# One run of score chunks a turn over six PSUM banks, with the other banks and the projection pieces dealt anew

## What is computed

```python
q = (x @ Wq).reshape(B, T, H, D)
k = (x @ Wk).reshape(B, T, H, D)
v = (x @ Wv).reshape(B, T, H, D)
q = _rmsnorm(q, q_rms_w)
k = _rmsnorm(k, k_rms_w)
...
gate = jax.nn.softplus(gate_logits)
bias = -dist[None, None] * omega_eff[None, :, None, None] * gate[:, :, None, :]
bias = jnp.where(causal[None, None], bias, -jnp.inf)
scores = jnp.einsum('bihd,bjhd->bhij', q, k) * scale + bias
attn = jax.nn.softmax(scores, axis=-1)
y = jnp.einsum('bhij,bjhd->bihd', attn, v).reshape(B, T, H * D)
return y @ Wproj
...
h = jnp.einsum('bei,eih->beh', jnp.concatenate([merged, ones], -1), w1)
h = jax.nn.gelu(h, approximate=False)
o = jnp.einsum('bej,ejo->beo', jnp.concatenate([h, ones], -1), w2)
```

## Time and profile before

| | us |
|---|---|
| median of 3 runs | 1491.17 |
| lowest and highest of them | 1486.17, 1493.72 |
| the profiled execution | 1487.67 |
| its span in the profile | 1485.9 |
| mean granted TensorE clock over the span | 0.973 of full |

### The profile page before, as it was taken

The page is one execution under the profiler, slowest core; times in us unless marked ns, Lnnn a source line. Parts: engine busy times, 40 slices in busy tenths (PEclk is TensorE's granted clock), DMA queues, the critical chain, the costliest instruction groups (busy, mean ns, idle before and its releaser), DMA issues.

```text
span 1485.9 us, 28161 instructions
## 1 busy us (share of the span) xinstructions
PE 1414.3 (95%) x9680; PEld 1089.7 (73%) x9680; DVE 990.7 (67%) x3164; ACT 914.2 (62%) x2292; POOL 165.5 (11%) x559
## 2 busy tenths in 40 slices
PE   3779999999999999999999999999998899999998
PEld 2566778777877877777777778777775778878787
DVE  5837885888587678757876885878587544444442
ACT  4637785878588577848866784877577433333332
POOL 4501110111011101101110110111011000000000
PEclk9779999999999999999999999999999999999999
DMA  5542322232223222323231322222230311111100
GB/s 202 193 161 79 99 94 80 80 121 71 93 67 108 83 85 76 114 67 102 96 98 61 99 94 80 80 97 84 75 94 6 87 39 40 40 39 40 39 15 29
DMA packets 88303, 122.90 MB, mean 83 GB/s; under 512 B 8561, under 2 KB 74466, under 8 KB 88162
## 3 DMA queue, kind: packets, MB, share of 16 engines
q1 hardware_dynamic: 85554, 116.35, 24.4%
q10 hardware_dynamic: 2608, 4.76, 0.9%
HBM read 101.69 MB, written 19.40 MB: 81 GB/s over the span
## 4 chain that ended last, share of the span: by engine, by line
PE 88%; ACT 4%; DVE 1%; issue 1%; DMA 0%; SPq 0%; ACTq 0%; DVEq 0%
PE at L797 18%; PE at L806 11%; PE at L882 10%; PE at L1467 8%; PE at L857 8%; PE at L923 7%; PE at L1503 6%; PE at L811 3%; PE at L892 2%; PE at L909 2%; PE at L849 2%; PE at L837 2%; PE at L1486 2%; PE at L842 2%; ACT L1063 1%; ACT probT L1054 1%
## 5 line engine op out<-in xcount | busy, mean ns | idle before, releaser
L1045 ACT ACTIVATE prob<-prob,low 128x512 f32<-128x512 f32 (+3 forms) x512 | 280.6, 550 | 70.5 <-DVE low L1178 70.5
L1178 DVE CUSTOM_DVE_ANT_0 prob<-at,mask 128x512 f32<-128x512 f32 (+3 forms) x512 | 220.4, 486 | 78.7 <-PE at L811 78.7
L1054 ACT ACTIVATE probT<-at 128x512 f32<-128x512 f32 (+1 forms) x256 | 131.5, 540 | 123.1 <-PE at L857 123.0
L806 PE MATMUL at<-kT,qT 64*128 64x512 f32 (+3 forms) x1024 | 194.0, 460 | 8.8 <-DVE up_lo L1231 5.0
L797 PE MATMUL at<-w_hi,cT_lo 128*128 128x386 f32 x512 | 197.3, 385 | 5.1 <-DVE area_raw L1127 4.3
L797 PE MATMUL at<-w_hi,cT_hi 128*128 128x386 f32 x512 | 174.8, 342 | 0.0
L797 PE MATMUL at<-w_lo,cT_hi 128*128 128x386 f32 x512 | 174.7, 341 | 0.0
L857 PEld LDWEIGHTS at<-ident,prob 128*128 128x128 f32 x1280 | 142.4, 141 | 40.0 <-issue 36.8
L857 PE MATMUL at<-ident,prob 128*128 128x128 f32 x1280 | 164.4, 275 | 2.1 <-DVE prob L1191 1.9
L1191 DVE TENSOR_SCALAR prob<-prob,rec 128x512 f32<-128x512 f32 (+3 forms) x512 | 163.3, 383 | 4.5
L882 PE MATMUL at<-probT,v 128*64 128x512 f32 (+3 forms) x1024 | 152.8, 440 | 0.1
(11 more groups left out here) (216 smaller groups left out, 2563.4 us busy)
## 6 DMA issues: line engine op xcount, KB each, us to landing
area_w<-in_L_ffn_w SPq DMA_DIRECT2D x64, 1024.0 KB, 5.6
bias<-in_L_ffn_w SPq DMA_DIRECT2D x160, 32.0 KB, 3.7
x_in<-in_L_attn_x SPq DMA_DIRECT2D x8, 512.0 KB, 5.8
xr<-in_L_attn_x SPq DMA_DIRECT2D x8, 512.0 KB, 4.0
eo_d<-eo SPq DMA_DIRECT2D x32, 128.0 KB, 1.8
x_d<-xr SPq DMA_DIRECT2D x8, 512.0 KB, 2.9
area_raw<-x_d SPq DMA_DIRECT2D x8, 512.0 KB, 4.0
out<-area_raw SPq DMA_DIRECT2D x8, 512.0 KB, 2.9
```

What stands on the lines that cost most here:

```text
L806: eng.matmul(bS[i][:, at:at + (c + 1) * P], qT[rows, c * P:(c + 1) * P], kT[rows, 0:(c + 1) * P], start=True, stop=False)
L1045: eng.activation(sl, sl, ACT.Exp, scale=-1.0, bias=low[:, i:i + 1], accum_out=den[:, i:i + 1]).then_inc(exp_done.sem, 1)
L1054: eng.activation(probT[h][:, x:y], bR[i][:, 0:y - x], ACT.Copy).then_inc(done.sem, 1)
L1178: eng.tensor_tensor_reduce(out=prob[s % 2][h][:, off[c]:off[c + 1]], in0=bS[i][:, at:at + (c + 1) * P], in1=mask[:, (NT - 1 - c) * P:T], s ...
```

## The change

All four score chunks of a turn stand in one run on TensorE (`all_scores`), over six banks: the three `bS` and the three `bR` (`bC`). The projection no longer shares a bank with them. The transposed probabilities of head 0 go to `bS`, those of head 1 to `bR`, and each waits until `lows` has emptied its bank of this turn's scores, not until the other head's copies are done. The values' result, the experts' products and the hidden rows take one `bS` bank each (`bY`, `bX`, `bH`). Projection piece 1 moves ahead of `turn_p1`, piece 2 ahead of `values`. VectorE and ScalarE are reordered to match. The run of scores now starts with the waits that `scores_210` had: for `add_bias`, `copy_expert_output` and `copy_hidden` of the turn before.

```diff
-        bY = bR[2]
-        bX = bS[2]
-        bS = bS + [bQ[0]]
+        bY, bX, bH = bS
+        bP = (bS, [bR[2], bR[0], bR[1]])
+        bC = bS + [bR[2], bR[0], bR[1]]
...
         place = {(3, 0): (0, 0), (3, 1): (1, 0), (1, 0): (2, 0), (1, 1): (3, 0),
-                 (2, 0): (1, 0), (2, 1): (0, 0), (0, 0): (1, 3 * P), (0, 1): (0, 3 * P)}
+                 (2, 0): (4, 0), (2, 1): (5, 0), (0, 0): (4, 3 * P), (0, 1): (5, 3 * P)}
...
-                def scores_3(s):
+                def all_scores(s):
                     eng.wait_ge(maxed.sem, maxed.at(s - 1))
-                    scores(3)
-
-                def scores_210(s):
+                    eng.wait_ge(y_done.sem, y_done.at(s - 2))
                     if begins_in(s - 1) is not None:
                         eng.wait_ge(biased.sem, biased.at(begins_in(s - 1)))
                     if s > 1 and ends_in(s - 1) is not None:
                         eng.wait_ge(eo_done.sem, eo_done.at(ends_in(s - 1)))
-                    eng.wait_ge(raw_D.sem, raw_D.at(s + 2 if s + 2 < NTURN else NTURN - 1))
-                    for n in jobs_at.get((s, 1), ()):
-                        eng.wait_ge(prep_done.sem, prep_done.at(n))
-                    scores(1)
-                    eng.wait_ge(maxed.sem, maxed.at(s, 2))
-                    if ends_in(s) is not None:
-                        eng.wait_ge(hidT_done.sem, hidT_done.at(ends_in(s)))
-                    scores(2)
-                    scores(0)
+                        eng.wait_ge(hidT_done.sem, hidT_done.at(ends_in(s - 1)))
+                    for c in (3, 1, 2, 0):
+                        scores(c)
...
                 def turn_p0(s):
                     eng.wait_ge(p_done.sem, p_done.at(s, 1))
                     for i in range(3):
+                        if s + 1 < NTURN:
+                            eng.wait_ge(maxed.sem, maxed.at(s + 1, i + 1))
                         turn_p(s, 0, i)
 
                 def turn_p1(s):
                     eng.wait_ge(p_done.sem, p_done.at(s, 2))
-                    eng.wait_ge(pt0_A.sem, pt0_A.at(s, 1))
-                    turn_p(s, 1, 0)
-                    eng.wait_ge(pt0_D.sem, pt0_D.at(s))
-                    turn_p(s, 1, 1)
-                    eng.wait_ge(pt0_A.sem, pt0_A.at(s, 2))
-                    turn_p(s, 1, 2)
+                    for i in range(3):
+                        if s + 1 < NTURN:
+                            eng.wait_ge(maxed.sem, maxed.at(s + 1, (4, 7, 8)[i]))
+                        turn_p(s, 1, i)
...
                 def hidden(m, s):
-                    eng.wait_ge(maxed.sem, maxed.at(s, 4))
+                    eng.wait_ge(maxed.sem, maxed.at(s, 2))
+                    eng.wait_ge(pt0_D.sem, pt0_D.at(s - 1))
...
                     if s > 0:
                         turn_p0(s - 1)
                     if s + 2 < NTURN:
                         eng.wait_ge(o_done.sem, o_done.at((s - 1) // HP - 1))
                         project(s + 2, 0)
                     prepare(s, 0)
+                    if s + 2 < NTURN:
+                        project(s + 2, 1)
+                    prepare(s, 1)
                     if s > 0:
                         turn_p1(s - 1)
                     if ends_in(s) is not None:
                         turn_hidden(ends_in(s), s)
                     if s + 2 < NTURN:
-                        project(s + 2, 1)
-                    prepare(s, 1)
-                    if s < NTURN:
-                        scores_210(s)
+                        project(s + 2, 2)
+                    prepare(s, 2)
                     if s > 0:
                         values(s - 1)
...
-                    if s < NTURN:
-                        eng.wait_ge(maxed.sem, maxed.at(s, 4))
-                    if s + 2 < NTURN:
-                        project(s + 2, 2)
-                    prepare(s, 2)
                     if s + 1 < NTURN:
+                        if s == 0:
+                            eng.wait_ge(maxed.sem, maxed.at(0, 8))
                         turn_q(s + 1)
```

More of the change, by code:

```diff
@@ L805, in scores @@
                         rows = slice(h * D, (h + 1) * D)
-                        eng.matmul(bS[i][:, at:at + (c + 1) * P], qT[rows, c * P:(c + 1) * P], kT[rows, 0:(c + 1) * P],
+                        eng.matmul(bC[i][:, at:at + (c + 1) * P], qT[rows, c * P:(c + 1) * P], kT[rows, 0:(c + 1) * P],
                                    start=True, stop=False)
@@ L810, in scores @@
                         rows = slice(h * D, (h + 1) * D)
-                        m = eng.matmul(bS[i][:, at:at + (c + 1) * P], qaug[rows, c * P:(c + 1) * P],
+                        m = eng.matmul(bC[i][:, at:at + (c + 1) * P], qaug[rows, c * P:(c + 1) * P],
                                        kaug[rows, 0:(c + 1) * P], start=False, stop=True)
                         m.then_inc(pe_s.sem, 1)
-                def scores_3(s):
+                def all_scores(s):
                     eng.wait_ge(maxed.sem, maxed.at(s - 1))
-                    scores(3)
-                def scores_210(s):
+                    eng.wait_ge(y_done.sem, y_done.at(s - 2))
                     if begins_in(s - 1) is not None:
@@ L955, in _ @@
                         eng.wait_ge(kaug_done.sem, kaug_done.at(s))
-                        scores_3(s)
+                        all_scores(s)
                     else:
                         eng.wait_ge(y_done.sem, y_done.at(s - 2))
+                        eng.wait_ge(eo_done.sem, eo_done.at(E - 1))
                     if s > 0:
@@ L1053, in copy_p @@
                     x, y = segT[i]
-                    eng.activation(probT[h][:, x:y], bR[i][:, 0:y - x], ACT.Copy).then_inc(done.sem, 1)
+                    eng.activation(probT[h][:, x:y], bP[h][i][:, 0:y - x], ACT.Copy).then_inc(done.sem, 1)
                 def copy_y(s):
@@ L1090, in _ @@
                         exps(s, 3)
+                        exps(s, 1)
+                    if s > 0:
+                        copy_p(s - 1, 0, 0)
+                        copy_p(s - 1, 0, 2)
                     prepare(s, 0)
+                    if s + 1 < NTURN:
+                        rsqrt(s + 1)
+                    if s + 2 < NTURN:
+                        take_raw(s + 2, 1)
+                    prepare(s, 1)
                     if s > 0:
@@ L1094, in _ @@
                         copy_p(s - 1, 1, 2)
-                    if s + 1 < NTURN:
-                        rsqrt(s + 1)
                     if s % 4 == 2:
                         exps(s, 3)
-                    prepare(s, 1)
-                    if s + 2 < NTURN:
-                        take_raw(s + 2, 1)
+                        exps(s, 1)
+                    if s < NTURN:
+                        exps(s, 2)
                     if s + 1 < NTURN:
                         gate(s + 1)
+                    if s + 2 < NTURN:
+                        take_raw(s + 2, 2)
+                    prepare(s, 2)
                     if s < NTURN:
-                        exps(s, 1)
-                        exps(s, 2)
                         exps(s, 0)
@@ L1178, in lows @@
                         eng.tensor_tensor_reduce(
-                            out=prob[s % 2][h][:, off[c]:off[c + 1]], in0=bS[i][:, at:at + (c + 1) * P],
+                            out=prob[s % 2][h][:, off[c]:off[c + 1]], in0=bC[i][:, at:at + (c + 1) * P],
                             in1=mask[:, (NT - 1 - c) * P:T], scale=-1.0, scalar=-LOWEST, op0=ALU.add, op1=ALU.min,
@@ L1200, in copy_p @@
                     x, y = segT[1]
-                    eng.tensor_copy(probT[h][:, x:y], bR[1][:, 0:y - x]).then_inc(done.sem, 1)
+                    eng.tensor_copy(probT[h][:, x:y], bP[h][1][:, 0:y - x]).then_inc(done.sem, 1)
                 def add_bias(m):
@@ L1251, in _ @@
                         lows(s, 3)
+                        lows(s, 1)
+                    if s + 1 < NTURN:
+                        mean_square(s + 1)
+                    if s < NTURN:
+                        lows(s, 2)
+                        lows(s, 0)
+                    if s + 2 < NTURN:
+                        take_raw(s + 2)
+                    prepare(s, 0)
                     if s > 0:
                         copy_p(s - 1, 0)
-                    if s + 2 < NTURN:
-                        take_raw(s + 2)
+                    prepare(s, 1)
                     if s + 1 < NTURN:
-                        mean_square(s + 1)
-                    prepare(s, 0)
+                        newton_step(s + 1)
                     if s > 0:
                         copy_p(s - 1, 1)
-                    if ends_in(s) is not None:
-                        copy_hidden(ends_in(s))
                     if s + 1 < NTURN:
-                        newton_step(s + 1)
                         gate_input(s + 1)
@@ L1267, in _ @@
                         gate(s + 1)
-                    prepare(s, 1)
-                    if s < NTURN:
-                        lows(s, 1)
```

(4 more changed lines are left out.)

21 lines of the change are left out of this document (8 added, 13 removed).

## The result

The changed kernel takes 1505.11 us (median of 4 runs, 1501.82 to 1507.73), the kernel before, beside it, 1488.99 (4 runs). The ratio is 1.0104, with a 95% interval of 1.0068 to 1.014: slower by 1.0%, 16.1 us. The forecast was 1502 and slower.

What follows compares the result with a forecast made beforehand. TensorE's own work bounds each turn; other engines count only where it waits. Plain turns -6.4, turns like 39 +7.8, GELU turns +17.3 and the end -8 give +10.7 us, 1502 on the median of 1491.17; range 1486 to 1519.

Steps and rivals of the forecast that it cites:

- What TensorE saves: Fewer costly changes of neighbour among TensorE's matmuls: 0.2 us saved in a turn, with 0 and 0.35 as ends.
- the rule that weight loads hide: Next tile's weights load during the current matmul, so neighbour changes cost nothing: saving 0, sum about 9 us higher.
- the joined run of scores: All score chunks in one run on TensorE: 3.06 us instead of 3.15 in two parts, 0.09 less.
- The new neighbours: On TensorE, values behind piece 2 and turn_q behind an expert: 0 to 0.1 us more each.
- The wait for the expert's sum: TensorE waits 0.72 us before the scores after each turn that ends an expert; a turn like 39 becomes 15.30.
- The wait for the hidden rows: In the GELU turn copy_hidden follows a late gate; TensorE waits 1.7 us before expert_output, the turn lasts 16.9 instead of 15.75.
- The 2.66 us for a table switch: Skill's price per ScalarE table switch; two would lengthen the GELU turn's chain by 2.1 us, the sum by 31.
- The loop: 32 plain turns -6.4 us, 15 turns like 39 +7.8, 15 GELU turns +17.3.
- The end of the loop: Turns 62 and 63: scores no longer wait for jobs, 1.7 us of waits come back; 8 us gained, between 4 and 10.
- The covers: Waits before turn_p0, turn_p1, values and turn_aug are fulfilled in time and cost nothing; thinnest at values, 0.3 us.
- The rival on the clock: Each GELU turn's 1.7 us wait brings half clock, as 5.0 us idle did: 26 us more, 1528; chance 0.05.
- The rival on the other side: ScalarE's gate at 10.3 makes copy_hidden ready when TensorE comes; GELU turn 15.30, sum -13, 1478; chance 0.10.

Runs made afterwards that it cites:

- the later pair of single runs: The changed kernel once more, unaltered, for a second trace, with the kernel before beside it: 1501.38 us against 1488.25.
- The experiment with the bank: Changed kernel with the experts' products in the bank of chunk 1 of head 0, hidden rows in that of chunk 3 of head 1: 1473.82 us.
- The early gate: Changed kernel with ScalarE's gate in the GELU turn right after the exponentials of chunk 3, ahead of chunks 1 and 2: 1477.4 us, ratio 0.9914.
- the experiment that moved the consumer: Changed kernel with VectorE's copy_hidden ahead of gate_input, norm and gate, ScalarE's order kept: 1487.91 us, ratio 0.9991.
- GpSimd's later work: Changed kernel with GpSimd's second-layer preparation waiting for the scores of turn 63 instead of the last projection: 1495.46 us, one run.
- the early-GELU experiment: Kernel before, old banks, with ScalarE's GELU ahead of the copies of head 0 in the GELU turn: 1517.96 us, one run.
- the experiment on piece 2: Changed kernel with projection piece 2 back behind the experts, its take_raw and prepare behind copy_y: 1565.88 us, one run.

## Why the prediction was right, and where it was off

The direction, the mechanism and the time (1502 for 1505.1) were right, and so was the chain in its steps. That the time is so close is in part luck. I forecast 10.7 us more than before; the medians differ by 16.1, and the later pair of single runs by 13.1. The forecast stood on a median of 1491.17 for the kernel before, which is 1488.99 with its fourth run, and two errors of the sum partly cancel: the loop was put 2.5 too high, the gain at the end 4.8 too high.

- **What TensorE saves.** Forecast 0.2 us a plain turn, measured 0.26 (14.54 to 14.28, the means of the plain turns of the loop without an output). By the rule that weight loads hide, of the Trainium skill (TensorE: Matmul & The Clock Gate, Part 2, Step-by-step), it would have been 0. The six steps of piece 1 behind piece 0 are 0.18 apart each, as I took. The term that was too small is the joined run of scores: it takes 2.95 us and not 3.06, since chunk 1 is also shorter behind chunk 3 than behind a projection (0.55 us from its start to that of chunk 2, instead of 0.66). The new neighbours (values behind piece 2, `turn_q` behind an expert) cost 0.08 and 0.05, 0.13 together, more than the 0.07 that my 0.2 left for them.
- **The wait for the expert's sum.** Forecast 0.72 us and a turn of 15.30, measured 0.77 and 15.34. The experiment with the bank takes it away and 25 us with it.
- **The wait for the hidden rows.** Forecast 1.7 us between 10.9 and 12.65, measured 1.51 between 11.0 and 12.56, and the turn 16.9 against 16.93. The forecast of ScalarE's gate, 12.0, was 11.93. The 2.66 us for a table switch of the Trainium skill (ScalarE: Activation LUTs, What ACT_TABLE_LOAD costs) did not show: both loads and the GELU again take 3.23 (745.32 to 748.55).
- **The loop** sums to +18.7 in the forecast and +16.25 in the trace. The other 31 plain turns saved 1.9 more than I took, and the GELU turns and their followers cost 1.2 more. The rest is turn 0, which my sum counted as a plain turn at -0.2: it went from 14.29 to 12.37. Before, `hidden` waited there for `lows` and half the clock followed, as the row and the window below show; now two waits of 1.41 and 0.64 us stand there, at full clock.

```profile
116.81 1.94 PE L892 MATMUL at<-area_w,tok 128*32 128x256 f32 x16 [2.61 <-DVE low L1178]
```

```profile
116.80:120.10 3.30, 3.29 (x20) 2.03 (x21) 3.16 (x14) 2.70 (x12) 0.78 (x4) 0.50 0.27 19
```

- **The end of the loop** is the term that was mis-sized. I took 8 us gained, the trace has 3.2: from the first scores of turn 62 to the second layer's first matmul 45.25 us before and 42.09 after. The long waits did go, but I had priced what comes back at 1.7. Behind turn 62 the run of scores waits 2.92 us for the expert's sum, instead of 0.77: the divide beside GpSimd's preparation takes 1.33 more, a job ahead of `copy_q` costs 0.2, and TensorE comes 0.6 earlier, since a job stands where piece 3 was. GpSimd's preparation starts 15.8 us into the turn, where it was 11.6 before and ran beside `lows`. And the clock fell here all the same, after idle times of 1.75 and 2.92 us. The second trace gained only 1.4 in this stretch, so 3.2 is not a firm number either. In the last pass `values` waits 2.04 for VectorE's copies behind the jobs.
- **The covers** that I cost at nothing held: no wait before `turn_p0`, `turn_p1`, and `values` in the loop. The rival on the clock did not come about: the loop's granted clock is 1.00, with fifteen idle times of 1.5 us in it.
- **The rival on the other side** asked for a gate at 10.3 or earlier. The early gate shows that it named the deciding point rightly: with the gate moved to 9.74, the kernel is 0.9% faster than before, at 1477; I had said 1478. As differences from the kernel before these are 10.6 us and 13, so the match of the times is partly chance. What was against it, the written order, was indeed all that kept it away.

Loop +16.25 and end -3.2 give +13.1; the medians differ by 16.1. The missing 3 us are less than what the same code scatters outside the loop; where they lie no run shows.

## What to carry to other kernels

When banks are dealt anew, each old wait moves with its bank, so ask for each where in the new order it is asked for and when its producer can be done: here a wait that had been idle at the middle of a turn became the turn's length at its start, and placing the bank 1.2 us later in the same run removed it. On an engine with a written order, one small result (here eight columns of a gate) placed behind long work delays everything that other engines queue behind it; move the producer, not one consumer, since the experiment that moved the consumer got back half. Add the hand-over to a cover before you trust it: here 0.3 us of cover were 0.07. And when TensorE is full, a kernel's length can be read turn by turn: the loop of the changed kernel repeats to 0.06 us in three traces (the third with GpSimd's later work), while its four runs scatter by 6.

## What the runs showed that I had not expected

- **The clock after short idle times.** Fifteen idle times of 1.5 us each in the loop left the granted clock at full (2.4 GHz), and did so again in the second trace. Idle times of 1.9 to 2.0 us in the early-GELU experiment were followed by a stretch at half (1.2 GHz) in six of fifteen turns and not in the other nine, at a cost of about 1.6 us each. Of fifteen idle times of 1.6 to 1.8 us in the experiment on piece 2 one was. And one of 1.75 us in turn 62, which all eight traces with the new banks have at the same place, was in six of them and not in two (the early gate and piece 2); in the changed kernel:

```profile
1157.35:1160.86 3.51, 3.51 (x19) 3.21 (x17) 2.65 (x9) 2.34 (x6) 0.00 (x0) 0.51 0.00 0
```

- **GpSimd and VectorE hold each other up.** The divide from SBUF to SBUF, four operations, takes 2.47 us instead of 1.14 beside GpSimd's two selections. Only the first two of the four are longer (0.92 instead of 0.42 us, 1.11 instead of 0.28), and each ends 0.1 to 0.2 us after the selection beside it, at 1168.52 and 1169.55, where the selections end at 1168.30 and 1169.46. The Trainium skill (SBUF — State Buffer, Who interferes with whom) says that a VectorE operation in a mode that uses two ports and a GpSimd operation take a shared pair of ports by turns, the later one waiting until the earlier has finished; the divide, a tensor_scalar, is of the kind it names. The trace agrees with that, and also with `lows` not slowing down; that the ports are the reason no run here shows by itself. It works the other way too: small operations of GpSimd's `augment`, 0.20 to 0.21 us each before, take 0.26 to 0.33 where they now run beside VectorE's divide.
- **The same code before the loop** took from 108.5 to 114.1 us in the traces of this study.
